# Folding the layer norms of a four-layer network into weights, a scaled turn and the FFN's outcome

## Time and profile before

| | us |
|---|---|
| median of 3 runs | 235.51 (235.11 to 235.87) |
| the profiled execution's own time | 235.9 |
| its span, first to last instruction | 233.9 |
| PE busy | 224.8 (96%) |
| DVE busy | 202.8 (87%) |
| ACT busy | 168.1 (72%) |
| POOL busy | 91.3 (39%) |
| chain of work that ended last | PE 80%, DVE 8%, ACT 7% |

### The profile page before, as it was taken

One profiled execution on the slowest core, in us unless ns is written; L12 is line 12 of the kernel. 1 busy time (PEld: TensorE's weight loads), 2 busy tenths in 40 slices (PEclk: granted clock), 3 DMA queues, 4 the chain that ended last, 5 costly groups with the idle time before them and its releaser, 6 DMA issues.

```text
span 233.9 us, 4615 instructions
## 1 busy us (share of the span) xinstructions
PE 224.8 (96%) x1494; PEld 173.6 (74%) x1494; DVE 202.8 (87%) x508; ACT 168.1 (72%) x498; POOL 91.3 (39%) x163
## 2 busy tenths in 40 slices
PE   7999898899999999999999999999999999999995
PEld 2797576567776677676866678888888888888885
DVE  3679888986998989999898878999999994999886
ACT  2267355799869987899979999567558766666660
POOL 6200215648895867276834849923000000000000
PEclk9999999999999999999999999999999999999999
DMA  6920000000320300020000313321110004322001
GB/s 178 355 70 4 0 0 0 1 3 0 98 85 3 92 0 3 0 92 1 3 0 4 90 28 127 121 48 45 45 46 0 3 0 149 123 68 69 0 3 45
DMA packets 9463, 11.71 MB, mean 50 GB/s; under 512 B 720, under 2 KB 6096, under 8 KB 9312
## 3 DMA queue, kind: packets, MB, share of 16 engines
q1 hardware_dynamic: 9008, 11.16, 15.1%
q10 hardware_dynamic: 432, 0.27, 0.4%
HBM read 10.87 MB, written 0.56 MB: 49 GB/s over the span
## 4 chain that ended last, share of the span: by engine, by line
PE 80%; DVE 8%; ACT 7%; issue 2%; DMA 1%; POOL 0%; SPq 0%; ACTq 0%; DVEq 0%
PE bank L960 7%; PE bank L936 7%; PE bank L1048 6%; PE bank L1051 6%; PE bank L1036 6%; PE bank L1049 6%; PE bank L1038 6%; PE bank L1037 6%; PE bank L985 5%; PE bank L894 3%; ACT early_prob L589 3%; PE bank L905 3%; PE bank L942 2%; PE bank L1093 2%; ACT probT L545 2%
## 5 line engine op out<-in xcount | busy, mean ns | idle before, releaser
L619 ACT ACTIVATE hb<-bank,pk 128x512 f32<-128x512 f32 x64 | 43.0, 702 | 21.2 <-PE bank L1038 21.0
L1526 DVE TENSOR_TENSOR hlo<-hb,hhi 128x512 fp32r<-128x512 f32 x64 | 45.1, 727 | 3.4 <-ACT hhi L622 2.3
L589 ACT ACTIVATE prob<-bank,negmax 128x192 f32<-128x192 f32 (+1 forms) x64 | 29.2, 497 | 5.1 <-DVE negmax L1476 5.0
L1476 DVE TENSOR_REDUCE negmax<-bank 128x2 f32<-128x384 f32 (+2 forms) x48 | 29.5, 634 | 3.1 <-PE bank L942 2.9
L435 POOL TENSOR_TENSOR w_lo<-w_raw,w_hi 128x256 fp32r<-128x256 f32 x32 | 25.3, 790 | 2.6
L1048 PE MATMUL bank<-hhi,w_hi 128*128 128x512 f32 (+2 forms) x68 | 25.9, 381 | 0.0
L1051 PE MATMUL bank<-hlo,w_hi 128*128 128x512 f32 (+2 forms) x68 | 25.8, 379 | 0.0
L1049 PE MATMUL bank<-hhi,w_lo 128*128 128x512 f32 (+2 forms) x68 | 25.8, 379 | 0.0
L1036 PE MATMUL bank<-xhi,w_hi 128*128 128x512 f32 x64 | 25.4, 396 | 0.0
L545 ACT ACTIVATE probT<-bank 128x512 f32<-128x512 f32 x38 | 22.9, 640 | 3.4 <-PE bank L960 1.8
L1038 PE MATMUL bank<-xhi,w_lo 128*128 128x512 f32 x64 | 25.0, 390 | 0.0
(11 more groups left out here) (160 smaller groups left out, 525.9 us busy)
## 6 DMA issues: line engine op xcount, KB each, us to landing
w_raw<-w SPq DMA_DIRECT2D x16, 256.0 KB, 3.0
comb_b<-routes SPq DMA_DIRECT2D x16, 256.0 KB, 3.2
pk<-packed SPq DMA_DIRECT2D x1, 1280.0 KB, 8.6
pk<-packed SPq DMA_DIRECT2D x1, 560.0 KB, 5.6
xs<-x SPq DMA_DIRECT2D x3, 128.0 KB, 2.9
out<-acc SPq DMA_DIRECT2D x3, 128.0 KB, 1.7
xs<-x ACTq DMA_DIRECT2D x1, 128.0 KB, 3.1
pk<-packed ACTq DMA_DIRECT2D x1, 68.0 KB, 2.5
```

Source lines behind the costliest of these rows:

```text
L589: last = nc.scalar.activation(prob_of(n, u)[:, of], lane[n][u % 2][:, of], ACT.Exp, bias=negmax[n][:, unit_query(u), h:h + 1], accum_out=s ...
L619: nc.scalar.activation(hb[blk % 2][:, j, :], h_bank[j][:, :], ACT.Relu, bias=bias).then_inc(h_ready, 1)
L1476: V.tensor_reduce(negmax[n][:, unit_query(u), heads[0]:heads[-1] + 1], lane[n][u % 2][:, :].rearrange("q (h k) -> q h k", h=len(heads))[:, ...
L1526: V.tensor_tensor(hlo[blk % 2][:, j, :], hb[blk % 2][:, j, :], hhi[blk % 2][:, j, :].bitcast(F32), ALU.subtract).then_inc(hlo_ready, 1)
```

## The change

It leaves the mean out of the tokens and takes it out of the weights, and it moves the factor rstd.

1. A new constant `centre` = I - 1/128 (128 more columns of the packed constants, 64 KB). On PE, products with it replace the weights of both attentions (q, k: one product of 512 columns for each layer; v: 128 columns for each) by centred ones: `centre_first` stands ahead of `group_stats(1, 0)`, `centre_rest` takes the place of the six `keep_clock` products. ACT copies the results back over the weights (`centred_weights`, four copies). The FFN's binarized weight is centred by one more product of 128 columns inside `values(0, 2)` and copied by DVE inside `copy_values(0, 2)`.
2. For norm 0 of samples 2, 3 and norm 2 of all samples, DVE's `norm` goes; POOL writes diag(rstd) into ht (`scales`, two instructions of 128x128 for each sample), and `turn` becomes a float32 product of t with that diagonal matrix.
3. For norm 1 (the FFN) `norm` goes, t itself is turned, and `add_bias` multiplies the outcome by rstd: two instructions of 128x128 instead of one of 128x256, with a wait for rstd.
4. Norm 0 of samples 0, 1 and norm 3 stay. The `after_norm` waits of POOL go, except those of norm 3.

```diff
+            def scales(j, n):
+                pool.wait_ge(ln_rstd[n % 2], normed(j, n))
+                for i in range(TT):
+                    last = G.tensor_scalar(ht[n][:, i, :], ident, rstd[n][:, i:i + 1], 1.0, ALU.mult, ALU.mult)
+                last.then_inc(ln_diag[n % 2], 1)
...
             masked_keys(0, 1)
-            after_norm(0, 3)
+            scales(0, 2)
+            scales(0, 3)
             binarized_weight()
...
             power(1, 1)
             power(1, 0)
-            after_norm(1, 0)
-            after_norm(1, 1)
             split_weights(2, 2)
...
             power(2, 1)
+            scales(2, 1)
             power(2, 0)
-            after_norm(2, 0)
-            after_norm(2, 1)
+            scales(2, 0)
...
+            def centred_weights():
+                act.wait_ge(centre_full, 1)
+                copy(pk[:, AT["aq"]:AT["av"]], two[0][0][:, :]).then_inc(centred, 1)
+                act.wait_ge(centre_full, 2)
+                copy(pk[:, AT["cq"]:AT["cv"]], two[1][0][:, :]).then_inc(centred, 1)
+                act.wait_ge(centre_full, 3)
+                copy(const("av"), two[3][1][:, 0:128])
+                copy(const("cv"), two[3][1][:, 128:256]).then_inc(centred, 1)
...
             def turn(j, n):
-                pe.wait_ge(ln_h[n % 2], normed(j, n))
+                if j == 1:
+                    pe.wait_ge(t_ready[n % 2], passed(0, n) + 1)
+                elif (j, n // 2) in SCALED_IN_TURN:
+                    pe.wait_ge(ln_diag[n % 2], scaled(j, n))
+                else:
+                    pe.wait_ge(ln_h[n % 2], written(j, n))
...
-                    last = nc.tensor.transpose(norm_bank(j, n)[:, i * 128:(i + 1) * 128], ht[n][:, i, :], ident)
+                    dst = norm_bank(j, n)[:, i * 128:(i + 1) * 128]
+                    if j == 1:
+                        last = nc.tensor.transpose(dst, t[n][:, i, :], ident)
+                    elif (j, n // 2) in SCALED_IN_TURN:
+                        last = mm(dst, t[n][:, i, :], ht[n][:, i, :], start=True, stop=True)
+                    else:
+                        last = nc.tensor.transpose(dst, ht[n][:, i, :], ident)
...
+            def centre_first():
+                pe.wait_ge(x1_ready, 1)
+                mm(two[0][0][:, :], const("centre"), pk[:, AT["aq"]:AT["av"]], start=True, stop=True
+                   ).then_inc(centre_full, 1)
+            def centre_rest():
+                pe.wait_ge(x1_ready, 2)
+                mm(two[1][0][:, :], const("centre"), pk[:, AT["cq"]:AT["cv"]], start=True, stop=True
+                   ).then_inc(centre_full, 1)
+                mm(two[3][1][:, 0:128], const("centre"), const("av"), start=True, stop=True)
+                mm(two[3][1][:, 128:256], const("centre"), const("cv"), start=True, stop=True
+                   ).then_inc(centre_full, 1)
...
             first_mix(3)
+            centre_first()
             group_stats(1, 0)
-            keep_clock(rest_a, 6)
+            centre_rest()
             squeeze(0)
...
             def values(a, n):
                 pe.wait_ge(k_parts_ready[n % 2], passed(a, n) + 1)
+                if (a, n) == FFN_WEIGHT_BESIDE:
+                    pe.wait_ge(w_eff_ready, 1)
+                    mm(lane[n][1][:, T:T + 128], const("centre"), w_eff[:, :], start=True, stop=True)
...
             def add_bias(n):
                 dve.wait_ge(ffn_full[n % 2], n // 2 + 1)
-                V.tensor_tensor(fy[n % 2][:, :, :], tiles(lane[n][2][:, T:2 * T]), tiles(const("fb")),
-                                ALU.add).then_inc(ffn_copied[n % 2], 1)
+                dve.wait_ge(ln_rstd[n % 2], normed(1, n))
+                for i in range(TT):
+                    last = V.scalar_tensor_tensor(
+                        fy[n % 2][:, i, :], lane[n][2][:, T + i * 128:T + (i + 1) * 128], rstd[n][:, i:i + 1],
+                        const("fb", i * 128, (i + 1) * 128), ALU.mult, ALU.add)
+                last.then_inc(ffn_copied[n % 2], 1)
```

More of the change, by code:

```diff
@@ L40 @@
     cq=256, ck=256, cv=128, co=128, causal0=64, causal1=128, headmask=8, router=8,
-    iota=8, b1=E * HC, b2=E,
+    centre=128, iota=8, b1=E * HC, b2=E,
 )
@@ L105, in build @@
         w_eff = sb("w_eff", [128, 128])
+        w_eff_centred = sb("w_eff_centred", [128, 128])
         cmv = sb("cmv", [128, B, 2])
@@ L192, in build @@
         w_mean_read, w_eff_step = sem("w_mean_read"), sem("w_eff_step")
+        centre_full, centred, w_eff_centred_ready = (
+            sem(n) for n in ("centre_full", "centred", "w_eff_centred_ready"))
         cs_ready, gs_ready, ve_ready, rstd_ready, hn_ready = (
@@ L203, in build @@
             sem(n) for n in ("sq_full", "spad_ready", "spad2_ready", "conv_full", "conv_ready", "x2_ready", "tok_full"))
-        ln_ve, ln_rstd, ln_h, lnT_full, lnT_ready = (
-            sems(n, LANES) for n in ("ln_ve", "ln_rstd", "ln_h", "lnT_full", "lnT_ready"))
+        ln_ve, ln_rstd, ln_h, ln_diag, lnT_full, lnT_ready = (
+            sems(n, LANES) for n in ("ln_ve", "ln_rstd", "ln_h", "ln_diag", "lnT_full", "lnT_ready"))
         ak_full, aq_full, k_hi_ready, q_hi_ready, k_parts_ready, q_lo_ready, atv_full = (
@@ L253, in normed, with written, scaled @@
             return LANE_NORMS.index((j, n // LANES)) + 1
+        FFN_WEIGHT_BESIDE = (0, 2)
+        NORMED_HERE = ((0, 0), (3, 0), (3, 1))
+        SCALED_IN_TURN = ((0, 1), (2, 0), (2, 1))
+        def written(j, n):
+            return NORMED_HERE.index((j, n // LANES)) + 1
+        def scaled(j, n):
+            return SCALED_IN_TURN.index((j, n // LANES)) + 1
         def passed(a, n):
@@ L382, in power @@
                 G.tensor_tensor(rstd[n][:, :], mv[n][:, :, 1], neghalf[:, 0:TT], ALU.pow).then_inc(ln_rstd[n % 2], 1)
+            def scales(j, n):
[3 more added lines that the diff above has]
+                last.then_inc(ln_diag[n % 2], 1)
             def after_norm(j, n):
-                pool.wait_ge(ln_h[n % 2], normed(j, n))
+                pool.wait_ge(ln_h[n % 2], written(j, n))
             def add_quantized(n):
@@ L494, in _ @@
             power(1, 2)
-            after_norm(1, 2)
-            after_norm(1, 3)
             split_weights(3, 2)
@@ L501, in _ @@
             power(2, 3)
+            scales(2, 3)
             power(2, 2)
-            after_norm(2, 2)
-            after_norm(2, 3)
+            scales(2, 2)
             split_weights(4, 0)
@@ L688, in _ @@
             first_probs_turned(3)
+            centred_weights()
             squeezed(0)
@@ L876, in product @@
                 if j == 1:
-                    pe.wait_ge(w_eff_ready, 1)
+                    pe.wait_ge(w_eff_centred_ready, 1)
                 for i in range(TT):
@@ L880, in product @@
                         last = mm(lane[n][2][:, T + i * 128:T + (i + 1) * 128], hT[n][:, i * 128:(i + 1) * 128],
-                                  w_eff[:, :], start=True, stop=True)
+                                  w_eff_centred[:, :], start=True, stop=True)
                     else:
@@ L885, in product @@
                 last.then_inc((ffn_full if j == 1 else lg_full)[n % 2], 1)
+            def centre_first():
[9 more added lines that the diff above has]
+                   ).then_inc(centre_full, 1)
             def project_keys(a, n):
+                pe.wait_ge(centred, 3)
                 pe.wait_ge(lnT_ready[n % 2], normed(2 * a, n))
@@ L1109, in squeeze @@
                 pe.wait_ge(hn_ready, B + n + 1)
+                if n == 3:
+                    pe.wait_ge(centred, 3)
                 mm(two[n][1][0:96, 0:T], const("squeeze"), hn[n][:, :], start=True, stop=True).then_inc(sq_full, 1)
@@ L1114, in convolve @@
                 pe.wait_ge(spad2_ready, n + 1)
+                if n < 2:
+                    pe.wait_ge(centred, n + 1)
                 for dy in range(3):
@@ L1468, in copy_values @@
                 dve.wait_ge(atv_full[n % 2], passed(a, n) + 1)
+                if (a, n) == FFN_WEIGHT_BESIDE:
+                    V.tensor_copy(w_eff_centred[:, :], lane[n][1][:, T:T + 128]).then_inc(w_eff_centred_ready, 1)
                 halves = vh[n][:, :, :].rearrange("k t (g x) -> k (t g) x", g=2)[:, :, 0:HG * HP]
@@ L1725, in _ @@
             copy_probs(0, 1, 0)
-            norm(0, 2)
-            norm(0, 3)
             largest(0, 1, 2)
@@ L1756, in _ @@
             largest(0, 3, 1)
-            norm(1, 1)
             norm_variance([0])
@@ L1760, in _ @@
             largest(0, 2, 2)
-            norm(1, 0)
             largest(0, 3, 2)
@@ L1774, in _ @@
             quantized_variance(0)
-            norm(2, 1)
-            norm(2, 0)
             copy_probs(0, 3, 4)
@@ L1796, in _ @@
             largest(1, 1, 1)
-            norm(1, 3)
             norm_variance([2])
@@ L1800, in _ @@
             largest(1, 1, 2)
-            norm(1, 2)
             largest(1, 0, 2)
@@ L1814, in _ @@
             quantized_variance(2)
-            norm(2, 3)
             copy_probs(1, 1, 4)
-            norm(2, 2)
```

(1 more changed line is left out.)

## The result

The changed kernel takes 238.16 us (median of 4 runs) against 235.69 for the one before: 1.0127 times as long, with a 95% interval of 1.0095 to 1.0159. Timed again beside the later experiments it took 237.83 against 235.57, 1.0090 (1.0069 to 1.0112). The ratios put it 3.0 and 2.1 us above the kernel before, the medians 2.47 and 2.26 us; what both intervals allow, 1.0095 to 1.0112, is 2.2 to 2.6 us. Forecast were 237.7 and +2.2. Of 79 runs of the kernel before, ten took 2.1 to 2.8 us longer than their median, and of the changed kernel's ten one took 240.68 and one 1246.81 us; no kept trace says why, so medians are compared, and the longest run is in no ratio.

What follows compares the result with a forecast made beforehand. PE was taken to bound the kernel: +0.87 between layers and +1.54 in the middle made +2.41 us, less 0.2 for gaps +2.2, so a median of 237.7 us. The range was 235.0 to 238.9, the forecast's own 236.9 to 238.5.

Steps and rivals of the forecast that it cites:

- What bounds the kernel: Middle, 45 to 142 us: PE or ACT fills each stretch, DVE none; time taken from DVE is worth little.
- The twelve product turns, +1.32: PE stretches of the middle: twelve transposes of norms 0 and 2 become products, 0.11 us more each, +1.32 us.
- The first centring product, +0.87: Between layers 0 and 1: centre_first ahead of group_stats(1, 0) delays DVE's list behind it by 0.87 us in full.
- centre_rest and ACT's copies, 0: Before squeeze(0): centre_rest replaces the idle products and ACT's four copies fit into its wait, 0 us.
- The FFN's weight, +0.22: Inside values(0, 2), near 64 us: the product that centres the FFN's weight adds 0.22 us on PE.
- The exps at 81.5, about 0: DVE's list before the exp at 81.50: longer add_bias +0.4, quantizing freed of POOL -0.49, about 0 us.
- Late diagonals, 0 with 0.1 to 0.4 us of margin: turn(2, 3), near 109 us: POOL's diagonals cost 0, 0.1 to 0.4 left; rival that they come late: 239.5, chance 0.12.
- The 0.2 that I took off for small gaps: PE stretches: earlier maxima may close small gaps between PE's pieces, 0.2 us off the sum of +2.41.
- The signs: gmv near 25.4, squeeze(0) near 27.2, ACT stretches equally long but 1.5 and 2.0 us later, DVE's share down 2 points.

Runs made afterwards that it cites:

- no_norms: The kernel before without the ten DVE norm calls that the change removes, other engines' work as before: 235.43 us, ratio 0.9975.
- turns_back: The changed kernel with DVE's norm and PE's transpose back for norm 0 (samples 2, 3) and norm 2: 236.96 us, ratio 1.0034.
- turn_twice: The kernel before with the twelve transposes of norm 0 (samples 2, 3) and norm 2 done twice: 236.87 us, ratio 1.0046.
- product_ahead: The kernel before with one unused float32 product of 512 columns put ahead of group_stats(1, 0): 236.32 us, ratio 1.0040.
- centre_behind: The changed kernel with the first centring product moved behind the group statistics' product: 237.24 us, ratio 1.0065.
- folded_cheap: The changed kernel with centre_first behind group statistics, FFN weight centred early, norm and transpose back for norm 0 (samples 2, 3) and norm 2: 235.64 us.

## Why the prediction was right, point by point

- **What bounds the kernel.** Right for PE and for what DVE's relief is worth: 0.36 us for 6.8 in no_norms, and every addition to PE's list in a PE stretch was paid, to within 0.16 us in the sum. Incomplete for the stretch from 69.97 to 83.27: ACT is the fullest there, as I wrote, but the chain is DVE's for 7.15 us of it, and I had only the exp at its end. DVE is the bound there, by the 0.36 us that no_norms gained before ACT took over. The change gained none of it, since its longer `add_bias` lies in this very part and takes up what the quantizing saved. And DVE stands at 81% in the last stretch of the earlier trace rows, not within the 83 to 94% that I gave for all.
- **The twelve product turns, +1.32.** Right in size: 1.31 between changed and turns_back, 1.16 for the same PE time without a product (turn_twice). Both figures hold shares of about 0.1 to 0.3 us that cancel, as said above.
- **The first centring product, +0.87.** Right: A grew by 0.87, and product_ahead shows it alone, 0.86.
- **centre_rest and ACT's copies, 0.** Right in place. ACT's copies had 0.64 us to spare; moved back by 0.87 us against the squeeze in centre_behind, they came onto the chain.
- **The FFN's weight, +0.22.** Too small: 0.40 by the chain, 0.34 when it was moved away. I priced DVE's copy as busy time and did not look at what stood behind it in DVE's list, the normalizing that the output product waits for.
- **The exps at 81.5, about 0.** Right, and for the reason given: DVE's part of the chain is 7.11 us for 7.15. The two `add_bias` took 0.61 each (I had 0.62), and the quantizing of sample 1 was freed of POOL:

```profile
73.51 0.73 POOL L457 TENSOR_TENSOR w_lo<-w_raw,w_hi 128x256 fp32r<-128x256 f32 x1
...
74.79 0.73 POOL L457 TENSOR_TENSOR w_lo<-w_raw,w_hi 128x256 fp32r<-128x256 f32 x1
...
75.61 0.61 DVE L1605 SCALAR_TENSOR_TENSOR fy<-bank,rstd,pk 128x128 f32<-128x128 f32 x2 [1.80 <-PE bank L921]
...
77.06 0.29 DVE L1639 TENSOR_SCALAR fz<-fz 128x256 f32<-128x256 f32 x1
```

  This is the timeline of the changed kernel. L1639 is the instruction that took 0.78 in the earlier trace rows; POOL's split had ended at 75.52, and it took 0.29. The next sample's L1639 runs beside a POOL instruction again and takes 0.78. That agrees with the lock between the two engines that the Trainium skill describes ("SBUF — State Buffer", "Who interferes with whom").
- **Late diagonals, 0 with 0.1 to 0.4 us of margin.** Right in the sum, wrong in the margin. The turn of sample 3 did wait for POOL, for 0.26 by the record of its weight load. It cost little, because before the change the same turn did not run at its full pace either: 0.40 in the chain for its two transposes, against 0.22 for each of the other pairs of norm 2. The product brought it to 0.71, so 0.31 more, of which 0.22 is the product's own. The lines are two of the changed kernel's timeline and one of the chain before:

```profile
110.32 0.72 POOL L403 TENSOR_SCALAR ht<-pk,rstd 128x128 f32<-128x128 f32 x2
...
111.09 0.52 PEld L906 LDWEIGHTS bank<-ht,t 128*128 128x128 f32 x4 [0.26 <-POOL ht L403]
...
109.35 0.40 PE bank L867 x2
```

- **The 0.2 that I took off for small gaps.** Wrong in sign for this kernel. The whole of the change is +2.72 inside the profile against a sum of 2.41, 0.31 more. The chains of both profiles place it. The first PE stretch grew by 0.94 where I had 0.66: 0.50 for the turns of samples 2 and 3 (I had 0.44), 0.40 for the FFN's weight (I had 0.22), 0.04 elsewhere. The other two grew by 0.45 and 0.47 (I had 0.44 each), the two ACT stretches by -0.06 and 0.02, and 0.03 came between gmv and 45 us. The 0.59 for four transposes held no gap that the longer turns closed.
- **The signs.** Counted from the same start, gmv came 0.87 later and the squeeze 0.87, as written. The two ACT stretches began 1.84 and 2.23 us later, where I had 1.5 and 2.0; the difference is the 0.3 above. DVE's share fell by 3 points, not 2.

## What to carry to other kernels

Cut the span where the chain changes its engine and ask which engine is full in each piece; a second engine at 90% need not be a second bound, and where it does hold the chain, relief of it is worth only the distance to the next engine, here 0.36 us of 6.8. The converse does not hold: the same engine loaded by 4.2 us more costs 3.3 at once, so "it would not help to relieve it" does not mean "it has room". And when work is moved ahead of an in-order list's next step, ask what the next step feeds: one product of 0.87 us ahead of a small one cost 0.86 to 0.87, and behind it 0.07 in centre_behind and at most 0.2 in folded_cheap.

## What the runs showed of the hardware that I had not expected

The length of layer 0, before any step that differs, varied by 1.4 us between profiles of kernels with the same steps there (21.50 to 22.91 for the start of its last product). The seven kernels that have `centre` among their constants, 64 KB more to load, lie between 21.50 and 22.25, the other five between 21.56 and 22.91. In the profiles of before and turn_twice, five idle products of 512 bf16 columns near 5.7 us were recorded with 2.29 us, in the changed kernel's second profile with 1.61 and in the other nine with 1.24. The granted clock was 1.00 in the window from 4.5 to 8.2 us, in the profile of before as in that of the changed kernel. I have no experiment that says why. It means that a difference under 1 us between two single profiles' spans can't be read without taking the start out.
